# A capped mixture-of-experts stage: fp32 products replaced by high and low fp32r parts, with the rows stationary and a ring of 4 raw weights in place of 8

## The chip, the cores and the metric

The kernel runs on one core of one Trainium2 chip. The metric is the device time of one execution in microseconds (us); lower is better. The core has a matrix engine (TensorE, "PE" in the views, with its weight loads shown apart as "PEld"), three elementwise engines (VectorE "DVE", ScalarE "ACT", GpSimd "POOL") and a queue engine that only issues transfers ("SP", shown as "SPq"). Each engine works through its own list of instructions in order; semaphores make one wait for another.

## The reference

The program is a decoder of six blocks. The change touches one part of the third, the routed experts of `_moe_forward`. 2048 tokens pick 4 of 32 experts each, and an expert takes at most C = 80 rows (1.25 x 2048 / 32); what is over is dropped. What is computed for each expert is:

```python
D = 512
I = 256
E = 32
...
            Xp = x[slots_token].reshape(E, C, d)
            G = jnp.einsum('ecd,edi->eci', Xp, W_gate)
            U = jnp.einsum('ecd,edi->eci', Xp, W_up)
            Y = jnp.einsum('eci,eid->ecd', jax.nn.silu(G) * U, W_down)
```

## The kernel before

The decoder is a row of stages; each ends with a barrier of all engines. The stage here is `capped_experts` (names with the prefix `m_`). The stage ahead of it, `late_routing` (prefix `cd_`), finishes the routing, writes the picked rows to `packed` in DRAM, and runs a part of the shared expert. In its place in the program it also calls `load_first`, which issues the raw weights of the first R experts, so that they arrive during `late_routing`. The stage behind it, `combine` (prefix `cc_`), gathers the results.

In `capped_experts` an expert e passes through one slot on each engine:

- SP loads its 80 rows of x (160 KB, `packed` into `xe`, a piece of the tile `moe_base`), and its three weights, gate and up (128x1024 floats, 512 KB each) and down (512 KB), into a ring of R = 8 places; it stores the 80 result rows (160 KB, from `ye`, another piece of `moe_base`). A place of the ring is filled again when PE has finished the expert that used it (`pe_o`), line 2233.
- PE turns x with 4 transposes (L2292), multiplies in fp32 with the weights as the stationary operand: 8 products of 128x128 by 80 columns for gate, 8 for up (L2298), and then, for the expert before, 2 products of the stationary h (80 columns) by 512 columns of the down weight (L2307). Each fp32 product is two instructions in the trace.
- DVE copies the turned x out of the matrix engine's memory (PSUM) (L2271) and multiplies silu(gate) by up (L2279).
- ACT computes silu (L2257) and copies the result out (L2251).
- POOL does nothing in this stage.

The engines run one slot ahead or behind each other by the calls `following` and `preceding`; PE's slot is `turn_x(e+1)`, gate(e), up(e), `down(e-1)`.

A later stage, `routed_experts` (prefix `n_`, lines 2362 to 2600), is not changed. It works on tiles of 128 rows and already has the form that the change brings here: an fp32 operand is split into a high part (a copy into the type fp32r, "CAST") and a low part (operand minus high part, by `tensor_tensor` with `subtract`), and `split_product` (L77) makes three fp32r products of them: low by high (L81 or L82), high by low, high by high (L83). On DVE and POOL such a subtraction of weights reads two operands in SBUF, the on-chip memory; those of x and h read one in PSUM and one in SBUF. The rows of that stage are used below as a price list.

## Time and profile before

| what | value |
|---|---|
| median of three runs | 3454.94 us (3453.34 to 3456.48) |
| the profiled execution: its time, and its span in the trace | 3457.22 us, 3455.4 us |
| first row load of the changed stage issued | at 1513.14 us of the span |
| last result store issued, and its landing | 1703.0, about 1705 us |
| time from one expert to the next in its middle | 5.57 us |

All times inside the trace are counted from the start of the span; the run's time is 1.8 us longer than the span. PE's granted clock is given as a share of its full 2.4 GHz; it has two levels here, 0.50 (1.2 GHz) and 1.00. "DMA share" is the mean busy share of the core's 16 transfer engines, GB/s what they moved.

### The profile page before, as it was taken

The numbers are of one execution on the slowest core, as the hardware profiler recorded it, in microseconds if no ns is written. First come the engines' busy times: TensorE is split into PE (matmuls) and PEld (weight loads), VectorE is DVE, ScalarE is ACT, GpSimd is POOL, SyncE is SP. The second block draws the span as 40 slices with busy tenths as digits, with TensorE's granted clock in tenths as the row PEclk, the third lists the DMA queues.
The fourth block names the chain that finished last, engine by engine and source line by source line (L and its number), as shares of the span: only waits on it lengthen the run. The fifth ranks groups of instructions, "written<-read, shape, count | busy, mean of one in ns | idle before, by whom it ended". The sixth has DMA issues, their size and how long they took to land. (4 is left out here: it accounts for less than half of the span.)

```text
span 3455.4 us, 58053 instructions
## 1 busy us (share of the span) xinstructions
PE 3126.9 (90%) x20720; PEld 2609.3 (76%) x20720; DVE 2117.7 (61%) x3794; ACT 1291.1 (37%) x3291; POOL 1456.0 (42%) x1470
## 2 busy tenths in 40 slices
PE   7999999999969999799896999699999999869991
PEld 5887878878847777677674777488888888758881
DVE  5667566676636667521285777566666678645556
ACT  2343333333346666401212333244444444324430
POOL 4554443344422333310173222355555556444445
PEclk9999999999979999899997999799999999979996
DMA  4001016023410111249573112311101001156664
GB/s 171 18 13 57 0 36 233 0 78 109 151 33 26 45 33 62 93 154 342 164 166 107 40 43 58 126 32 35 35 11 49 11 24 45 43 200 223 224 222 158
DMA packets 137869, 317.13 MB, mean 92 GB/s; under 512 B 18425, under 2 KB 30457, under 8 KB 135538
## 3 DMA queue, kind: packets, MB, share of 16 engines
q1 hardware_dynamic: 120194, 274.61, 23.5%
q0 software_dynamic: 15360, 36.25, 4.0%
...
## 5 line engine op out<-in xcount | busy, mean ns | idle before, releaser
L398 POOL TENSOR_TENSOR a_sq<-a_tq,a_sinq 128x256 f32<-128x256 f32 x128 | 150.4, 1195 | 359.4 <-DVE a_tq L474 358.1
L398 POOL TENSOR_TENSOR a_sk<-a_tk,a_sink 128x256 f32<-128x256 f32 x128 | 123.9, 987 | 90.0 <-DVE a_tk L474 90.0
L364 ACT COPY a_probT<-bank 128x512 f32<-128x512 f32 x64 | 37.5, 586 | 329.0 <-PE bank L713 329.0
L411 POOL TENSOR_TENSOR e_sk<-e_tk 128x512 f32<-128x512 f32 x64 | 66.5, 1039 | 205.5 <-DVE e_tk L501 205.5
L353 ACT ACTIVATE e_prob<-bank,e_nb,e_rq 128x128 f32<-128x128 f32 x256 | 113.8, 455 | 86.6 <-DVE e_nb L575 86.6
L348 ACT ACTIVATE a_sm<-a_sm,a_nmax 128x128 f32<-128x128 f32 x256 | 99.9, 391 | 122.3 <-DVE a_nmax L570 122.3
L952 ACT ACTIVATE b_prob<-bank,b_nb 128x128 f32<-128x128 f32 x512 | 139.1, 386 | 13.6 <-DVE b_nb L1148 13.4
L1046 POOL TENSOR_TENSOR d_prob<-d_prob,d_nmax 128x1024 f32<-128x1024 f32 x32 | 63.9, 1998 | 181.5 <-DVE d_nmax L1143 181.5
L2478 POOL TENSOR_TENSOR n_wu_lo<-nw_wu,n_wu_hi 128x1408 fp32r<-128x1408 f32 x23 | 74.0, 3219 | 136.5 <-DVE n_wu_hi L2522 136.5
L496 DVE TENSOR_TENSOR a_kr<-a_kr,a_sk 128x512 f32<-128x512 f32 x64 | 66.5, 1039 | 89.0 <-POOL a_sk L398 89.0
L1145 DVE TENSOR_REDUCE b_nmax<-bank 128x8 f32<-128x1024 f32 x64 | 77.9, 1218 | 67.6 <-PE bank L1289 63.5
L81 PE MATMUL bank<-a_wq_hi,a_x_lo 128*128 128x512 f32 x256 | 107.4, 419 | 7.3 <-DVE a_wq_lo L214 7.2
L943 ACT COPY b_probT<-bank 128x512 f32<-128x512 f32 x128 | 78.3, 612 | 89.7 <-PE bank L1298 89.6
L81 PE MATMUL bank<-e_wo_hi,e_z_lo 128*128 128x512 f32 x256 | 107.4, 420 | 3.1 <-DVE e_z_lo L538 3.1
L81 PE MATMUL bank<-a_wo_hi,a_z_lo 128*128 128x512 f32 x256 | 106.1, 415 | 2.9 <-DVE a_z_lo L538 2.9
L386 POOL TENSOR_TENSOR a_x_lo<-a_xall,a_x_hi 128x512 fp32r<-128x512 f32 x64 | 89.8, 1403 | 41.4 <-ACT a_x_hi L320 41.4
L413 POOL TENSOR_TENSOR e_sq<-e_tq 128x512 f32<-128x512 f32 x64 | 66.6, 1040 | 96.4 <-DVE e_tq L505 96.4
L81 PE MATMUL bank<-a_wk_hi,a_x_lo 128*128 128x512 f32 x256 | 100.9, 394 | 6.7 <-DVE a_wk_lo L214 6.7
L364 ACT COPY e_probT<-bank 128x512 f32<-128x512 f32 x64 | 37.5, 586 | 180.0 <-PE bank L713 180.0
L572 DVE TENSOR_REDUCE e_nmax<-bank 128x4 f32<-128x512 f32 x64 | 44.2, 690 | 96.2 <-PE bank L697 96.2
L2483 POOL TENSOR_TENSOR n_wd_lo<-nw_wd,n_wd_hi 128x1024 fp32r<-128x1024 f32 (+1 forms) x46 | 85.4, 1876 | 39.5 <-ACT n_wd_hi L2451 39.5
L83 PE MATMUL bank<-e_wo_hi,e_z_hi 128*128 128x512 f32 x256 | 102.0, 399 | 0.0
...
## 6 DMA issues: line engine op xcount, KB each, us to landing
...
```

Of the source, the lines that this page charges most:

```text
L81: nc.tensor.matmul(ps, a_lo, b_hi, start=start, stop=False)
L83: return nc.tensor.matmul(ps, a_hi, b_hi, start=False, stop=stop)
L348: step = nc.scalar.activation(prob[:, j, :], sm[:, j, :], ACT.Exp, bias=nmax[:, j:j + 1], accum_out=rsum[:, j:j + 1])
L353: step = nc.scalar.activation(prob[:, j, :], pS[:, P * j:P * j + P], ACT.Exp, bias=nb[:, j:j + 1], scale=rq[:, par, j:j + 1], accum_out=rs ...
L364: nc.scalar.copy(probT[:], pP[:, :]).then_inc(act_pt, 1)
L386: sub = nc.gpsimd.tensor_tensor(x_lo[:, par].rearrange("p c t -> p (c t)"), xall[:, b, :], x_hi[:, par].rearrange("p c t -> p (c t)").bitc ...
L398: step = nc.gpsimd.tensor_tensor(o, i, s, ALU.mult)
L943: nc.scalar.copy(probT[:, s // 2 % 2, s % 2], pP[:, :]).then_inc(act_pt, 1)
L952: step = nc.scalar.activation(prob[:, p % 2, i], pS[:, i // H, P * (i % H):P * (i % H) + P], ACT.Exp, bias=nb[:, p % 2, i:i + 1], scale=SCALE)
L1145: nc.vector.tensor_reduce(nmax[:, p], scores, AX.X, ALU.max, negate=True).then_inc(v_nm, 1)
L2478: nc.gpsimd.tensor_tensor(lo["u"][:, w], raw["u"][:, w], hi["u"][:, w].bitcast(F32), ALU.subtract).then_inc(g_u, 1)
L2483: sub = nc.gpsimd.tensor_tensor(o, x, y.bitcast(F32), ALU.subtract)
```

## The change

- `CappedWeights` holds a ring of R = 4 places in place of 8. Gate and up stand side by side in one array (`in_c_wgu`), so that one transfer of 1 MB brings both (8 KB in a row for each partition, where it was twice 4 KB). `load_first` brings 4 experts.
- ACT copies both halves of the joined weight and the down weight into fp32r (three copies of 128x1024 for each expert), and also x, h and the results. DVE subtracts for the low parts of both halves, of x and of h. POOL subtracts for the low part of the down weight.
- PE holds the rows as the stationary operand (80 columns) and moves 512 columns of weight: `up` is 4 x 3 products, `down` 2 x 3. The result has rows on partitions, so h is turned by two transposes more (`turn_h`).
- The place of a weight in the ring is filled again once its low part is made (`v_up`, `g_down`), one slot earlier than PE's use of it.
- All slots are written out one by one (no loop on the chip). `gate` and `h` share one piece of `moe_base` (`spare`).

```diff
--- before.py
+++ after.py
@@ -2176,153 +2176,226 @@
 class CappedWeights:
 
 
-    NE, F, R = 32, 256, 8
+    NE, F, R = 32, 256, 4
 
     def __init__(self, st, w_dram):
         self.w_dram = w_dram
...
+        self.up = st.sbuf("up", [P, self.R, C, 2 * self.F])
+        self.down = st.sbuf("down", [P, self.R, self.F // P, D])
+        self.up_in = [st.sem(f"up_in{n}") for n in range(self.R)]
+        self.down_in = [st.sem(f"down_in{n}") for n in range(self.R)]
+
+    def load_up(self, sp, e):
+        n = e % self.R
+        sp.dma_start(self.up[:, n], self.w_dram["wgu"][e]).then_inc(self.up_in[n], 16)
+
+    def load_down(self, sp, e):
+        n = e % self.R
+        sp.dma_start(self.down[:, n], self.w_dram["wd"][e]).then_inc(self.down_in[n], 16)
 
     def load_first(self, sp):
...
+        for e in range(self.R):
+            self.load_up(sp, e)
+            self.load_down(sp, e)
+
+
+def capped_experts(nc, psum, ident, packed, result, zero, weights, xe, ye, spare):
 
     NE, CAP, F, R = weights.NE, 80, weights.F, weights.R
...
+    FC, HALF = F // P, C // 2
     with ExitStack() as ctx:
         st = Stage(nc, ctx, "m")
-        pX, pG, pU, pO = psum[0:2], psum[2:4], psum[4:6], psum[6:8]
...
+        pX, pU, pH, pO = psum[0:2], psum[2:4], psum[4:6], psum[6:8]
+        up_hi, up_lo = (st.sbuf(n, [P, 2, C, 2 * F], F32R) for n in ("up_hi", "up_lo"))
+        down_hi, down_lo = (st.sbuf(n, [P, 2, FC, D], F32R) for n in ("down_hi", "down_lo"))
+        x_hi, x_lo = (st.sbuf(n, [P, 2, C, CAP], F32R) for n in ("x_hi", "x_lo"))
+        gate = h = spare.rearrange("p (n f) -> p n f", n=2)
+        h_hi, h_lo = (st.sbuf(n, [P, FC, CAP], F32R) for n in ("h_hi", "h_lo"))
         x_in = [st.sem(f"x_in{n}") for n in range(R)]
         y_out = [st.sem(f"y_out{n}") for n in range(2)]
...
+        z_out, pe_x, pe_u, pe_h, pe_o = st.sems("z_out", "pe_x", "pe_u", "pe_h", "pe_o")
+        act_x, act_up, act_down, act_g, act_h, act_y = st.sems("act_x", "act_up", "act_down", "act_g", "act_h", "act_y")
+        v_x, v_up, v_h, v_hl, g_down = st.sems("v_x", "v_up", "v_h", "v_hl", "g_down")
         block = ctx.enter_context(nc.Block())
+
+        def part(half):
+            return slice(HALF * half, HALF * half + HALF)
 
         @block.sync
         def _(sp):
...
+            def load_x(e):
+                sp.dma_start(xe[:, e % R, :], packed[e]).then_inc(x_in[e % R], 16)
+
+            def store(e):
+                sp.wait_ge(act_y, done(e))
+                sp.dma_start(result[0:NE * CAP].rearrange("(e r) d -> e r d", r=CAP)[e], ye[:, e % 2, :]).then_inc(y_out[e % 2], 16)
+
+            def follow(e):
+                if e + R < NE:
+                    sp.wait_ge(pe_x, done(e))
+                    load_x(e + R)
+                    sp.wait_ge(v_up, done(2 * e + 1))
+                    weights.load_up(sp, e + R)
 
             for n in range(2):
                 sp.sem_inc(y_out[n], 16)
...
+            for e in range(R):
+                load_x(e)
             sp.dma_start(result[NE * CAP:NE * CAP + 1, :], zero[0:1, :]).then_inc(z_out, 16)
...
-                    sp.wait_ge(pe_o, done(R * i + n))
-                    load(i + 1, n)
...
+            follow(0)
+            for e in range(NE):
+                follow(e + 1)
+                if e + R < NE:
+                    sp.wait_ge(g_down, done(e))
+                    weights.load_down(sp, e + R)
+                if e:
+                    store(e - 1)
+            store(NE - 1)
             sp.wait_ge(z_out, 16)
             for n in range(2):
                 sp.wait_ge(y_out[n], landed(NE // 2))
 
         @block.scalar
         def _(act):
...
+            head_start(act, act_x, act_up, act_down, act_g, act_h, act_y)
+
+            def take_x(e):
+                act.wait_ge(pe_x, done(e))
+                if e >= 2:
+                    act.wait_ge(pe_u, done(2 * (e - 2) + 1))
+                nc.scalar.copy(x_hi[:, e % 2], pX[e % 2][:, 0:C * CAP].rearrange("p (c t) -> p c t", c=C)).then_inc(act_x, 1)
+
+            def split_up(e, half):
+                act.wait_ge(weights.up_in[e % R], landed(e // R))
+                if e >= 2:
+                    act.wait_ge(pe_u, done(2 * (e - 2) + half))
+                nc.scalar.copy(up_hi[:, e % 2, part(half)], weights.up[:, e % R, part(half)]).then_inc(act_up, 1)
+
+            def split_down(e):
+                act.wait_ge(weights.down_in[e % R], landed(e // R))
+                act.wait_ge(pe_o, done(e - 2))
+                nc.scalar.copy(down_hi[:, e % 2], weights.down[:, e % R]).then_inc(act_down, 1)
+
+            def take_h(e):
+                act.wait_ge(pe_h, done(e))
+                act.wait_ge(pe_o, done(e - 1))
+                nc.scalar.copy(h_hi[:], pH[e % 2][:, 0:FC * CAP].rearrange("p (c t) -> p c t", c=FC)).then_inc(act_h, 1)
+
+            def take_y(e):
                 act.wait_ge(pe_o, done(e))
...
+                act.wait_ge(y_out[e % 2], landed(e // 2))
+                nc.scalar.copy(ye[:, e % 2, :], pO[e % 2][0:CAP, :]).then_inc(act_y, 1)
+
+            for half in range(2):
+                split_up(0, half)
+            take_x(0)
+            for half in range(2):
+                split_up(1, half)
+            for e in range(NE):
+                if e + 1 < NE:
+                    take_x(e + 1)
+                split_down(e)
+                if e + 2 < NE:
+                    split_up(e + 2, 0)
+                act.wait_ge(pe_u, done(2 * e + 1))
+                act.wait_ge(pe_h, done(e - 2))
+                nc.scalar.activation(gate[:, e % 2], pU[e % 2][0:CAP, 0:F], ACT.Silu).then_inc(act_g, 1)
+                if e + 2 < NE:
+                    split_up(e + 2, 1)
+                take_h(e)
+                if e:
+                    take_y(e - 1)
+            take_y(NE - 1)
+
+        @block.gpsimd
+        def _(pool):
+            head_start(pool, g_down)
+            for e in range(NE):
+                pool.wait_ge(act_down, done(e))
+                nc.gpsimd.tensor_tensor(down_lo[:, e % 2], weights.down[:, e % R], down_hi[:, e % 2].bitcast(F32), ALU.subtract).then_inc(g_down, 1)
 
         @block.vector
         def _(dve):
...
-                nc.vector.tensor_copy(xT[:, n % 2], pX[n % 2][:, 0:C * CAP].rearrange("p (c t) -> p c t", c=C)).then_inc(v_x, 1)
...
+            head_start(dve, v_x, v_up, v_h, v_hl)
+
+            def take_x_lo(e):
+                dve.wait_ge(act_x, done(e))
+                nc.vector.tensor_tensor(x_lo[:, e % 2], pX[e % 2][:, 0:C * CAP].rearrange("p (c t) -> p c t", c=C),
+                                        x_hi[:, e % 2].bitcast(F32), ALU.subtract).then_inc(v_x, 1)
+
+            def split_up_lo(e, half):
+                dve.wait_ge(act_up, done(2 * e + half))
+                nc.vector.tensor_tensor(up_lo[:, e % 2, part(half)], weights.up[:, e % R, part(half)],
+                                        up_hi[:, e % 2, part(half)].bitcast(F32), ALU.subtract).then_inc(v_up, 1)
+
+            def take_h_lo(e):
+                dve.wait_ge(act_h, done(e))
+                nc.vector.tensor_tensor(h_lo[:], pH[e % 2][:, 0:FC * CAP].rearrange("p (c t) -> p c t", c=FC),
+                                        h_hi[:].bitcast(F32), ALU.subtract).then_inc(v_hl, 1)
+
+            split_up_lo(0, 0)
+            take_x_lo(0)
+            split_up_lo(0, 1)
+            split_up_lo(1, 0)
+            for e in range(NE):
+                if e:
+                    take_h_lo(e - 1)
+                if e + 1 < NE:
+                    take_x_lo(e + 1)
+                    split_up_lo(e + 1, 1)
                 dve.wait_ge(act_g, done(e))
...
+                nc.vector.tensor_tensor(h[:, e % 2], gate[:, e % 2], pU[e % 2][0:CAP, F:2 * F], ALU.mult).then_inc(v_h, 1)
+                if e + 2 < NE:
+                    split_up_lo(e + 2, 0)
+            take_h_lo(NE - 1)
 
         @block.tensor
         def _(pe):
...
+            head_start(pe, pe_x, pe_u, pe_h, pe_o)
+
+            def turn_x(e):
+                pe.wait_ge(x_in[e % R], landed(e // R))
+                pe.wait_ge(v_x, done(e - 2))
                 for c in range(C):
...
+                    last = nc.tensor.transpose(pX[e % 2][:, CAP * c:CAP * c + CAP], xe[:, e % R, P * c:P * c + P], ident[0:CAP, 0:CAP])
                 last.then_inc(pe_x, 1)
 
-            def up(ps, w, n, sem):
+            def up(e):
+                pe.wait_ge(v_x, done(e))
+                pe.wait_ge(v_h, done(e - 2))
+                for c in range(C):
+                    if c % HALF == 0:
+                        pe.wait_ge(v_up, done(2 * e + c // HALF))
+                    last = split_product(nc, pU[e % 2][0:CAP, :], x_hi[:, e % 2, c, :], x_lo[:, e % 2, c, :],
+                                         up_hi[:, e % 2, c, :], up_lo[:, e % 2, c, :], start=c == 0, stop=c == C - 1)
+                    if c % HALF == HALF - 1:
+                        last.then_inc(pe_u, 1)
+
+            def turn_h(e):
+                pe.wait_ge(v_h, done(e))
+                pe.wait_ge(v_hl, done(e - 2))
                 for f in range(FC):
-                    for c in range(C):
-                        last = nc.tensor.matmul(ps[n % 2][:, CAP * f:CAP * f + CAP], w[:, n, c, P * f:P * f + P],
-                                                xT[:, n % 2, c, :], start=c == 0, stop=c == C - 1)
...
+                    last = nc.tensor.transpose(pH[e % 2][:, CAP * f:CAP * f + CAP], h[:, e % 2, P * f:P * f + P], ident[0:CAP, 0:CAP])
+                last.then_inc(pe_h, 1)
+
+            def down(e):
+                pe.wait_ge(v_hl, done(e))
+                pe.wait_ge(g_down, done(e))
                 pe.wait_ge(act_y, done(e - 2))
                 for f in range(FC):
...
+                    last = split_product(nc, pO[e % 2][0:CAP, :], h_hi[:, f, :], h_lo[:, f, :],
+                                         down_hi[:, e % 2, f, :], down_lo[:, e % 2, f, :], start=f == 0, stop=f == FC - 1)
                 last.then_inc(pe_o, 1)
 
...
-                pe.wait_ge(w_in[n], 48 * (i + 1))
...
+            turn_x(0)
+            for e in range(NE):
+                if e + 1 < NE:
+                    turn_x(e + 1)
+                up(e)
+                if e:
+                    down(e - 1)
+                turn_h(e)
+            down(NE - 1)
 
 
 class RoutedWeights:
@@ -2874,7 +2947,7 @@
                 weights = CappedWeights(Stage(nc, routed, "cw"), w)
                 late_routing(nc, "cd", psum, router, weight, early, weights.load_first)
                 capped_experts(nc, psum, ident, packed1.rearrange("(e r) d -> e r d", r=80), result1, zero, weights,
-                               base[0:80, B - weights.R:B], base[0:80, EARLY:EARLY + 2])
+                               base[0:80, B - weights.R:B], base[0:80, EARLY:EARLY + 2], base[0:80, EARLY + 2])
             combine(nc, "cc", base, result1, router.rows, weight, x2, 4, rest, staged_d.fetch)
         narrow_attention(nc, "d", banks, ident, lambda b: steps[0][b], lambda b: steps[1][b], of("d_"), 16, PLAN_4, staged_d, head_d, causal=True, ahead=fetch_e)
         with ExitStack() as moe:
@@ -2983,7 +3056,7 @@
     return {
         "c_rw": by_chunk(i["L0_ffn_router_w"].T), "c_sg": by_chunk(i["L0_ffn_shared_gate"].T),
         "c_su": by_chunk(i["L0_ffn_shared_up"].T), "c_sd": by_chunk(i["L0_ffn_shared_down"].T),
...
+        "c_bias": i["L0_ffn_e_bias"], "c_iota": iota, "c_wgu": by_expert(np.concatenate([i["L0_ffn_W_gate"], i["L0_ffn_W_up"]], axis=2)),
         "c_wd": by_expert(i["L0_ffn_W_down"]),
         "f_rw": by_chunk(i["L1_ffn_gate_w"].T), "f_iota": iota, "f_wg": by_expert(i["L1_ffn_gate_proj"].transpose(0, 2, 1)),
         "f_wu": by_expert(i["L1_ffn_up_proj"].transpose(0, 2, 1)), "f_wd01": by_expert(down[:, :2 * P]),
```

The order of the instructions shows three places. First DVE, from the start of the stage on; before, it has two short instructions for each expert (`m_xT` the turned x, `m_h` the product with silu).

```order
-L2271 COPY m_xT<-bank 128x320 x2
-L2279 TENSOR_TENSOR m_h<-m_gate,bank 128x160
...
-L2271 COPY m_xT<-bank 128x320
-L2277 REGISTER_ALU
-L2279 TENSOR_TENSOR m_h<-m_gate,bank 128x160
```

In the changed kernel it has five (`m_up_lo` is a half of the low part of gate and up, `m_x_lo` and `m_h_lo` those of x and h, `moe_base<-moe_base,bank` the product with silu).

```order
1006 L2347 TENSOR_TENSOR moe_base<-moe_base,bank 80x256
1007 L2328 TENSOR_TENSOR m_up_lo<-cw_up,m_up_hi 128x1024
1008 L2333 TENSOR_TENSOR m_h_lo<-bank,m_h_hi 128x160
1009 L2323 TENSOR_TENSOR m_x_lo<-bank,m_x_hi 128x320
1010 L2328 TENSOR_TENSOR m_up_lo<-cw_up,m_up_hi 128x1024
1011 L2347 TENSOR_TENSOR moe_base<-moe_base,bank 80x256
```

So the second half of the low part of expert e+1 stands ahead of the product of expert e. Next ACT, in one slot in the middle of the changed stage (before it has the silu and the copy of the result alone).

```order
597 L2266 CAST m_x_hi<-bank 128x320
598 L2277 CAST m_down_hi<-cw_down 128x1024
599 L2272 CAST m_up_hi<-cw_up 128x1024
600 L2302 ACTIVATE moe_base<-bank 80x256
601 L2272 CAST m_up_hi<-cw_up 128x1024
602 L2282 CAST m_h_hi<-bank 128x160
603 L2287 COPY moe_base<-bank 80x512
```

Three large copies came in, two of them ahead of the silu and one behind it. Last SP, where the first weights are loaded and the stage begins; first before (the loads of the eight experts, of which the last stands here), then of the change.

```order
-L2190 DMA cw_wg<-in_c_wg 128x1024
-L2190 DMA cw_wu<-in_c_wu 128x1024
-L2190 DMA cw_wd<-in_c_wd 128x1024
...
 L1912 UNCONDITIONAL_BRANCH
-L2214 UNCONDITIONAL_BRANCH
-L2217 DMA moe_base<-packed 80x512 x8
-L2230 DMA result<-all_zero 1x512
```

```order
142 L2224 UNCONDITIONAL_BRANCH
143 L2227 DMA moe_base<-packed 80x512 x4
144 L2244 DMA result<-all_zero 1x512
145 L2227 DMA moe_base<-packed 80x512
146 L2190 DMA cw_up<-in_c_wgu 128x2048
147 L2227 DMA moe_base<-packed 80x512
148 L2190 DMA cw_up<-in_c_wgu 128x2048
149 L2194 DMA cw_down<-in_c_wd 128x1024
150 L2227 DMA moe_base<-packed 80x512
```

The weights of experts 4 and on are now issued from the first slot on, where before expert 8 waited for the end of expert 0.

## Rows read from the trace of the kernel before

**Rows 1.** The page: span, and busy time of each engine.

```profile
span 3455.4 us, 58053 instructions
PE 3126.9 (90%) x20720; PEld 2609.3 (76%) x20720; DVE 2117.7 (61%) x3794; ACT 1291.1 (37%) x3291; POOL 1456.0 (42%) x1470
```

**Rows 2.** Busy time by stretch: the loads ahead, then the stage in four parts.

```profile
core 0: us, PE busy (x) PEld busy (x) DVE busy (x) ACT busy (x) POOL busy (x), PEclk, DMA share, GB/s
1455.00:1480.00 25.00, 22.93 (x144) 20.61 (x144) 9.14 (x42) 3.44 (x6) 11.67 (x12) 0.81 1.03 396
1513.00:1533.00 20.00, 17.34 (x79) 15.89 (x80) 2.12 (x5) 0.61 (x2) 0.00 (x0) 0.57 0.25 67
1535.00:1560.00 25.00, 25.00 (x186) 20.46 (x185) 3.25 (x8) 3.84 (x9) 0.00 (x0) 1.00 0.98 321
1560.00:1670.00 110.00, 110.00 (x789) 87.53 (x788) 16.26 (x40) 17.69 (x40) 0.00 (x0) 1.00 1.00 341
1670.00:1702.00 32.00, 32.00 (x217) 24.24 (x216) 3.89 (x10) 5.00 (x11) 0.00 (x0) 1.00 0.11 35
```

**Rows 3.** Timeline of PE over one expert: start, duration, instruction.

```profile
1561.53 0.44 PE L2292 MATMUL bank<-all_ident,moe_base 80*128 80x80 f32 x4
1561.81 1.95 PE L2298 MATMUL bank<-m_xT,cw_wg 128*128 128x80 f32 x16
1563.59 1.95 PE L2298 MATMUL bank<-m_xT,cw_wu 128*128 128x80 f32 x16
1565.38 1.88 PE L2307 MATMUL bank<-cw_wd,m_h 128*80 128x512 f32 x4
1567.10 0.30 PE L2292 MATMUL bank<-all_ident,moe_base 80*128 80x80 f32 x2
```

**Rows 4.** Issues of the stage's small transfers, KB each, median us to landing.

```profile
moe_base<-packed SPq DMA_DIRECT2D x32, 160.0 KB, 5.7
result<-moe_base SPq DMA_DIRECT2D x32, 160.0 KB, 8.4
```

**Rows 5.** Timeline of PE in the stage with prefix n_: split products.

```profile
3161.89 0.39 PE L82 MATMUL bank<-n_wd_lo,n_h_hi 128*128 128x512 f32 x1
3162.12 0.40 PE L83 MATMUL bank<-n_wd_hi,n_h_hi 128*128 128x512 f32 x1
3162.35 0.39 PE L81 MATMUL bank<-n_wd_hi,n_h_lo 128*128 128x512 f32 x1
```

**Rows 6.** Groups by shape: busy us, mean ns; idle before and releaser.

```profile
L2450 ACT CAST n_wd_hi<-nw_wd 128x1024 fp32r<-128x1024 f32 x23 | 24.4, 1062 | 0.0
L2433 ACT CAST n_x_hi<-bank 128x512 fp32r<-128x512 f32 x46 | 27.0, 586 | 152.9 <-PE bank L2555 152.9
L2438 ACT CAST n_h_hi<-bank 128x256 fp32r<-128x256 f32 x46 | 16.9, 368 | 3.8 <-PE bank L2562 3.8
L2459 ACT ACTIVATE n_gate<-bank 128x352 f32<-128x352 f32 x46 | 21.4, 464 | 65.0 <-PE bank L83 65.0
L2251 ACT COPY moe_base<-bank 80x512 f32<-80x512 f32 x32 | 18.6, 581 | 105.8 <-PE bank L2307 80.9 <-DMA result<-moe_base 24.8
L2500 DVE TENSOR_TENSOR n_x_lo<-bank,n_x_hi 128x512 fp32r<-128x512 f32 x46 | 31.8, 691 | 33.5 <-ACT n_x_hi L2433 33.4
L2505 DVE TENSOR_TENSOR n_h_lo<-bank,n_h_hi 128x256 fp32r<-128x256 f32 x46 | 19.2, 418 | 35.3 <-ACT n_h_hi L2439 35.3
L2483 POOL TENSOR_TENSOR n_wd_lo<-nw_wd,n_wd_hi 128x1024 fp32r<-128x1024 f32 x23 | 56.7, 2464 | 39.5 <-ACT n_wd_hi L2451 39.5
```

**Rows 7.** Timelines of POOL and DVE, n_ stage: two pairs that overlap.

```profile
3107.06 3.24 POOL L2478 TENSOR_TENSOR n_wu_lo<-nw_wu,n_wu_hi 128x1408 fp32r<-128x1408 f32 x1 [5.56 <-DVE n_wu_hi L2522]
3108.66 3.12 DVE L2517 TENSOR_TENSOR n_wg_lo<-nw_wg,n_wg_hi 128x1408 fp32r<-128x1408 f32 x1
3292.15 3.22 POOL L2478 TENSOR_TENSOR n_wu_lo<-nw_wu,n_wu_hi 128x1408 fp32r<-128x1408 f32 x1 [5.55 <-DVE n_wu_hi L2522]
3294.50 2.35 DVE L2517 TENSOR_TENSOR n_wg_lo<-nw_wg,n_wg_hi 128x1408 fp32r<-128x1408 f32 x1
```

**Rows 8.** Timeline of ACT, n_ stage: instructions back to back.

```profile
3152.77 0.37 ACT L2438 CAST n_h_hi<-bank 128x256 fp32r<-128x256 f32 x1
3153.02 0.28 ACT L2439 CAST n_h_hi<-bank 96x128 fp32r<-96x128 f32 x1
3153.18 1.06 ACT L2450 CAST n_wd_hi<-nw_wd 128x1024 fp32r<-128x1024 f32 x1
```

82 lines of the change are left out of this document (removed).

## The prediction

> **What bounds the kernel now.** I read the page first [rows 1]: PE is busy for 90% of the span, which says only that a change of PE's work can count. Then the busy time by stretch over the changed stage [rows 2]. The reader is to see that from 1535 to 1702 us PE is busy in every microsecond at the full clock, while DVE and ACT have 16 and 18 us of work in 110. The first 20 us are different: the clock stands at 0.57 of full on the mean, that is mostly at 1.2 GHz, behind the idle time at the barrier. The timeline of one expert [rows 3] shows PE with no gap: transposes 0.28 us, gate 1.78, up 1.79, down 1.72, and the next expert starts 5.57 us after this one. So the stage is bound by PE.
>
> The same rows show a second thing that is nearly full. From 1560 to 1670 us the DMA share is 1.00 at 341 GB/s. An expert moves 3 x 0.524 MB of weights and 2 x 0.164 MB of rows, 1.90 MB, and 1.90 / 5.57 us is 341 GB/s. The issues [rows 4] show that a row load of 160 KB lands after 5.7 us and a store after 8.4: they stand behind weights. PE never waits for a weight only because a ring of 8 lies in between. The transfers can do more where they carry weights alone (396 GB/s at share 1.03, 1455 to 1480 us) and did less at 321 [rows 2].
>
> **What PE's work costs after.** Six fp32 groups go; 12 + 6 products of 512 columns come. Such a product in the n_ stage starts 0.23 us after the one before it [rows 5]; 18 of them are 4.14 us. The x transposes stay at 0.28, the two of h are half of that, 0.14. With some 0.2 for restarts after a change of type (an estimate: the nearest row is none, so 0 to 0.4), PE needs 4.75 us for an expert, 0.82 less than 5.57. If nothing else bound, 32 x 0.82 = 26 us would go. That is the upper end of what can be gained.
>
> **What ACT does after** [rows 6]. Three copies of 128x1024 at 1.06 are 3.19. For x (320 columns) and h (160) I go along the line through 586 ns at 512 and 368 ns at 256 (0.85 ns a column): 0.42 and 0.29. Silu of 256 columns, between 464 ns at 352 and less: 0.38. The copy of the result 0.58. Together 4.86; but an instruction with nothing to wait for starts some 0.11 before the end of the one ahead (3153.18 + 1.06 against the next at 3154.13; [rows 8] show 3153.02 under 3152.77 + 0.37), so 7 of them hold the engine for about 4.1. ACT fits under 4.75.
>
> **What DVE and POOL do after, and each to the other.** The low parts of x and h have an operand in PSUM: 0.49 and 0.32 by the line through 691 and 418 ns; the product 0.42. The low parts of weights have both in SBUF. [Rows 7] show the same 128x1408 subtraction with 3.12 and with 2.35 us. The first runs beside POOL's for 3107.06 + 3.24 - 3108.66 = 1.64 us, the second for 3292.15 + 3.22 - 3294.50 = 0.87; 3.12 - 1.64 and 2.35 - 0.87 are both 1.48. So DVE gets nothing done there while POOL's subtraction runs, and then needs 1.48. For 1024 columns that is 1.08, with the start-up of 0.15 that the 691 ns for 512 columns leave at the same rate 1.23. POOL's own instruction takes 2.46 on the mean, 2.38 undisturbed. The Trainium skill says the same under "SBUF — State Buffer", section "SBUF: two separate sides": the pair of ports that both use is an exclusive lock for a whole instruction, taken by a DVE instruction with two SBUF inputs too; by that rule a DVE sum without the lock would be too small, and the trace agrees.
>
> DVE alone needs 2 x 1.23 + 0.49 + 0.32 + 0.42 = 3.7. If POOL's 2.38 falls wholly on it, 6.1; if it starts just when DVE turns to x and h (0.8 of cover), 5.3. What is queued behind it decides: the second half of the next expert's low part stands ahead of this expert's product with silu, for that product PE's `turn_h` waits, and for PE everything. In a slot of 4.75 there is room: after silu(e) DVE has the product, half one, h and x, half two, 3.7 in all, and POOL's subtraction can only start after ACT's copy of the down weight, about 3.2 us behind the silu (1.06 + 0.29 + 0.58 + 0.42 + 1.06 less the overlaps). Walking two slots with these numbers: in the first POOL finds DVE on half two, starts at 3.8 and ends at 6.2, so the next slot's half one starts about 1 us late, h and x follow, and there POOL comes first: half two starts after it, some 2.4 late, and that slot grows by 1 to 1.5 us. Then it begins again. Slots of 4.75 and of 5.8 to 6.0 in turn: 5.3 on the mean. I take 5.3; the bounds are 4.75 (POOL always in a gap) and 5.75 (it falls into the chain each time).
>
> **The transfers after.** The bytes of an expert are the same, in rows of 8 KB for two thirds of the weights. 28 experts' weights instead of 24 now move inside the stage: 28 x 1.573 + 32 x 0.328 = 54.5 MB, 160 us at 341 GB/s. They start 4 us into the stage, not 21, and a stage of 32 x 5.3 = 170 us holds them; they bind first at 54.5 / 170 = 320 GB/s, which the row 1535 to 1560 just reaches (321). I cost them at nothing in the sum and keep 300 to 396 GB/s as the bounds. The stores lie behind more waiting bytes than before, and ACT must have them landed two experts later (10.6 us against 8.4 measured): narrow, but enough. The lighter `load_first` takes 6.3 MB out of the stretch 1455 to 1480, where PE works on the shared expert; I find no wait there that I can price and take 0, at most 2 us gained. The loop written out costs nothing by itself: other stages of this program are written out too.
>
> **The sum.** Before, the stage runs from 1513.1 (first row load) to 1705 (last store landed), 191.9 us. After:
> - rows land at about 1515.5; transposes at the low clock, x_hi 0.42, x_lo 0.49 and the way between them: first product at 1517.5;
> - to about 1533 PE has the low clock, as now. 15.5 us at 2 x 4.56 an expert is 1.7 experts;
> - 30.3 experts at 5.3: 160.6 us, to 1693.6;
> - the last expert's h parts (0.29 + 0.32 and the ways), down 1.38, copy 0.58, store and landing 2.3: 5.7 us, to 1699.3.
>
> That is 5.7 us before 1705. The profiled execution took 3457.2 and would take 3451.5; it lies 2.3 above the median of the runs, so the median comes to 3454.9 - 5.7 = 3449.2. I say 3449. A measurement of this kernel tells 0.2%, 6.9 us, from no change: the likeliest time lies just inside that.
>
> **The rivals.**
> - POOL's subtraction mostly finds a gap (half two is ready early, and the ways between engines may shift the phase). Then PE's 4.75 holds: 30.3 x 0.55 = 16.7 less, 22 us gained in all; but 54.5 MB at 341 from 1517 on end at 1677, and the last expert needs two slots and the end, some 14 us more: 1691, 14 us gained. 3441, down to 3433 if transfers run near 396. For it: DVE has 3.7 of 4.75. Chance 0.25.
> - It finds the chain each time: 5.75 an expert, 30.3 x 0.45 = 13.6 more than the sum, 8 us slower than before, 3463. That is the case on the other side; it decides when the mean slot passes 5.5. Chance 0.15.
> - The transfers fall to 300 GB/s, because row stores and loads mix with more queued weights: 182 us from 1517 is 1699, and about 9 for the last expert: 1708, 3 us slower; at 290, 9 slower. 3458 to 3464. Against it: 341 over 110 us, and larger rows. Chance 0.10.
> - The sum's own case, 5.15 to 5.5 an expert: 4 us more to 6 us less than said, 3444 to 3455. Chance 0.50.
>
> **How the numbers follow.** Within 0.2% are 3448.0 to 3461.9. Of the sum's case 0.20 lies below that, 0.30 inside; of the first rival 0.23 below, 0.02 inside; of the second 0.05 inside, 0.10 above; of the third 0.05 and 0.05. Faster 0.43, same 0.42, slower 0.15; I move 0.04 from same to slower for what the written-out code and the shared port may do beyond these cases: 0.43, 0.38, 0.19. The range goes from 3434 (most of the first rival) to 3464 (the upper ends of the other two).
>
> **What would show it.** Right: PE busy near 90% of the stage, split products 0.23 apart, the halves of the low part at 1.23 alone and up to 3.5 us beside POOL, in turns; PE's idle time in front of `turn_h`, released by the product on DVE; first result slots at the low clock as before. Wrong: PE waiting for `up_lo` behind a late weight (the transfers bind), ACT waiting long for a landed store, POOL's instruction far from 2.4, the clock falling to 1.2 GHz in the middle because of PE's waits (then 9 us an expert, and all of this is void), or slots of one length, 4.75 or 5.75.

## The result, and the profile after

| what | before | after |
|---|---|---|
| median (lowest to highest) of 6 runs each | 3454.88 us (3452.93 to 3458.06) | 3439.23 us (3435.96 to 3442.04) |
| ratio, 95% interval | | 0.9958 (0.9946 to 0.997) |
| profiled execution, its span | 3457.22, 3455.4 us | 3438.98, 3436.8 us |

The changed kernel is faster by 15.7 us in the medians, 10 to 19 us by the interval: twice to three times the 5.7 us forecast, inside the range, below the likeliest case's own 3444 to 3455. Of the runs told of below, one of the six of e11_change_again took 4008 us at a granted clock of 0.73; such an execution is left out of every median and ratio here. The two profiled executions are 18.6 us of span apart. Put down by stretch, with the issues of SP as marks (the first weight load, the first row load, the last result store, the load of `d_wo` in the stage behind `combine`):

| stretch | before | after | difference |
|---|---|---|---|
| start to the first weight load | 1448.9 | 1447.1 | -1.8 |
| to the first row load (`late_routing`) | 64.2 | 61.2 | -3.0 |
| to the last result store (`capped_experts`) | 189.9 | 173.7 | -16.2 |
| to the load of `d_wo` in the next stage | 145.7 | 146.2 | +0.5 |
| the rest | 1606.7 | 1608.5 | +1.8 |

Below, "the stage" is the third row, and "a slot" is the time from one expert's silu on ACT to the next one's, read from the timeline of ACT. The page after, against [rows 1]:

```profile
span 3436.8 us, 57141 instructions
PE 3093.7 (90%) x20208; PEld 2559.9 (74%) x20208; DVE 2239.6 (65%) x3890; ACT 1400.5 (41%) x3451; POOL 1550.9 (45%) x1502
```

It says little: PE has 33 us less to do, the other three have 95 to 122 us more, nearly all of it beside PE. The busy time by stretch says more (columns as in [rows 2]):

```profile
1510.00:1515.00 5.00, 3.48 (x13) 2.39 (x14) 3.55 (x4) 3.70 (x6) 0.00 (x0) 0.59 0.48 139
1515.00:1520.00 5.00, 4.08 (x17) 2.34 (x16) 3.13 (x5) 3.43 (x6) 3.31 (x1) 0.72 1.00 347
1520.00:1525.00 5.00, 5.00 (x27) 3.37 (x26) 4.00 (x6) 4.46 (x8) 2.98 (x1) 1.00 0.96 357
1560.00:1650.00 90.00, 80.34 (x415) 52.64 (x414) 83.75 (x88) 74.72 (x122) 49.60 (x18) 1.00 1.01 367
```

Two things are to be seen. In the middle of the stage PE is no longer the full engine: it is busy for 80.3 of 90 us, DVE for 83.8. And the clock is full from about 1517.8 on (the 0.72 of the second row is 0.50 up to there and 1.00 behind it), some 9 us after the first row load; before, it was full at 1532.9, 20 us after ([rows 2] show 0.57 from 1513 to 1533). The waits between 1505 and 1700 us name who waits for whom (engine and line, what it waited for: us in total, times, longest):

```profile
POOL m_down_lo L2315 <- ACT m_down_hi L2277: 104.7, 32, 34.1
PE bank L2378 <- DVE moe_base L2347: 17.0, 11, 1.6
DVE moe_base L2347 <- ACT moe_base L2302: 13.5, 21, 2.5
PE bank L2360 <- DMA moe_base<-packed: 4.4, 1, 4.4
```

PE waits 11 times in the 31 slots, up to 1.6 us, at `turn_h` (L2378) for DVE's product with silu (L2347). No row has PE or ACT waiting for a weight or a store. The slots are 4.57, 4.57 and 6.39 us, again and again: 5.18 on the mean (5.14 in the table of the runs, which takes in the first and last slots). One long slot in the timeline of DVE:

```profile
1600.61 0.42 DVE L2347 TENSOR_TENSOR moe_base<-moe_base,bank 80x256 f32<-80x256 f32 x1 [0.70 <-ACT moe_base L2302]
1600.95 2.31 DVE L2328 TENSOR_TENSOR m_up_lo<-cw_up,m_up_hi 128x1024 fp32r<-128x1024 f32 x1
1603.81 1.21 DVE L2328 TENSOR_TENSOR m_up_lo<-cw_up,m_up_hi 128x1024 fp32r<-128x1024 f32 x1
1605.19 0.42 DVE L2347 TENSOR_TENSOR moe_base<-moe_base,bank 80x256 f32<-80x256 f32 x1 [0.17 <-ACT moe_base L2302]
1605.52 2.84 DVE L2328 TENSOR_TENSOR m_up_lo<-cw_up,m_up_hi 128x1024 fp32r<-128x1024 f32 x1
...
1608.92 3.00 DVE L2328 TENSOR_TENSOR m_up_lo<-cw_up,m_up_hi 128x1024 fp32r<-128x1024 f32 x1
1611.84 0.41 DVE L2347 TENSOR_TENSOR moe_base<-moe_base,bank 80x256 f32<-80x256 f32 x1
```

And of POOL, over the same time:

```profile
1599.28 2.89 POOL L2315 TENSOR_TENSOR m_down_lo<-cw_down,m_down_hi 128x1024 fp32r<-128x1024 f32 x1 [3.98 <-ACT m_down_hi L2277]
1603.86 3.42 POOL L2315 TENSOR_TENSOR m_down_lo<-cw_down,m_down_hi 128x1024 fp32r<-128x1024 f32 x1 [1.68 <-ACT m_down_hi L2277]
1608.43 2.41 POOL L2315 TENSOR_TENSOR m_down_lo<-cw_down,m_down_hi 128x1024 fp32r<-128x1024 f32 x1 [1.15 <-ACT m_down_hi L2277]
```

POOL's instruction ends at 1602.17, 1607.28 and 1610.84; DVE's halves beside it end at 1603.26, 1608.36 and 1611.92, each 1.08 to 1.09 us later. Where DVE was first (1603.81 against 1603.86), DVE takes 1.21 and POOL 3.42, that is 2.4 and the 1.0 that it stood. In the first slot half two just slips in ahead of POOL. In the second everything is shifted by what POOL took from half one, POOL comes first, half two ends at 1611.92, and the product behind it starts 2.1 us after silu has ended (silu from 1609.34 for 0.38, in the timeline of ACT). That is the long slot. After it POOL's work falls where DVE has time, and the cycle begins again. The groups of these instructions (busy us, mean ns | idle time ahead of them, releaser):

```profile
L2328 DVE TENSOR_TENSOR m_up_lo<-cw_up,m_up_hi 128x1024 fp32r<-128x1024 f32 x64 | 122.3, 1912 | 2.3 <-ACT m_up_hi L2272 2.3
L2315 POOL TENSOR_TENSOR m_down_lo<-cw_down,m_down_hi 128x1024 fp32r<-128x1024 f32 x32 | 92.7, 2897 | 104.7 <-ACT m_down_hi L2277 104.7
L2272 ACT CAST m_up_hi<-cw_up 128x1024 fp32r<-128x1024 f32 x64 | 66.9, 1049 | 10.5 <-PEq L50 10.0 <-PE bank L83 0.4
L2347 DVE TENSOR_TENSOR moe_base<-moe_base,bank 80x256 f32<-80x256 f32 x32 | 13.2, 413 | 13.6 <-ACT moe_base L2302 13.5
```

### The profile page after: what moved, and what is told of

Same layout as the page of the kernel before. It is cut to its first block and busy times, and to the rows that moved or that the text cites. A ratio compares the mean times of both kernels' runs of the same rounds, so it can differ in the third digit from the quotient of the medians.

```text
span 3436.8 us, 57141 instructions
## 1 busy us (share of the span) xinstructions
PE 3093.7 (90%) x20208; PEld 2559.9 (74%) x20208; DVE 2239.6 (65%) x3890; ACT 1400.5 (41%) x3451; POOL 1550.9 (45%) x1502
## 5 line engine op out<-in xcount | busy, mean ns | idle before, releaser
L2315 POOL TENSOR_TENSOR m_down_lo<-cw_down,m_down_hi 128x1024 fp32r<-128x1024 f32 x32 | 92.7, 2897 | 104.7 <-ACT m_down_hi L2277 104.7
L2328 DVE TENSOR_TENSOR m_up_lo<-cw_up,m_up_hi 128x1024 fp32r<-128x1024 f32 x64 | 122.3, 1912 | 2.3 <-ACT m_up_hi L2272 2.3
```

What stands on the lines that cost most here:

```text
L2315: nc.gpsimd.tensor_tensor(down_lo[:, e % 2], weights.down[:, e % R], down_hi[:, e % 2].bitcast(F32), ALU.subtract).then_inc(g_down, 1)
L2328: nc.vector.tensor_tensor(up_lo[:, e % 2, part(half)], weights.up[:, e % R, part(half)], up_hi[:, e % 2, part(half)].bitcast(F32), ALU.sub ...
```

## The experiments

All with their profiles; each ratio is to the kernel before on the same chip, with its 95% interval. "Rows" is the stretch from the first weight load to the first row load.

| run | median us | ratio (interval) | rows | stage | mean slot |
|---|---|---|---|---|---|
| the change | 3439.23 | 0.9958 (0.9946 to 0.997) | 61.2 | 173.7 | 5.14 |
| e1_no_down_lo | 3429.97 | 0.9947 (0.993 to 0.9964) | 61.2 | 168.3 | 4.97 |
| e2_halves_together | 3427.74 | 0.9948 (0.9931 to 0.9964) | 61.3 | 168.0 | 4.94 |
| e3_down_on_dve | 3429.82 | 0.9945 (0.9926 to 0.9964) | 61.1 | 171.8 | 5.09 |
| e4_before_ring4 | 3452.46 | 1.0011 (1.0 to 1.0022) | 61.0 | 191.5 | 5.74 |
| e5_fp32_rows | 3445.22 | 0.9983 (0.9974 to 0.9993) | 61.1 | 186.8 | 5.54 |
| e6_rows_4k | 3435.63 | 0.9956 (0.9939 to 0.9973) | 61.1 | 173.7 | 5.14 |
| e7_quarter_loads | 3414.10 | 0.9899 (0.988 to 0.9918) | 61.1 | 155.3 | 4.55 |
| e8_quarter_change | 3432.42 | 0.9948 (0.9929 to 0.9967) | 61.4 | 173.7 | 5.14 |
| e9_four_results | 3428.76 | 0.9918 (0.9905 to 0.9931) | 63.9 | 162.9 | 4.79 |
| e10_halves_again | 3436.73 | 0.9937 (0.9921 to 0.9953) | 63.7 | 169.0 | 4.97 |
| e11_change_again | 3439.72 | 0.9955 (0.9942 to 0.9968) | 63.6 | 173.0 | 5.13 |
| e12_before_again | one run, 3455.0 | | 63.8 | 190.3 | 5.71 |

The kernel before had a median of 3447.0, 3449.7 and 3456.7 us in the three groups e1 to e4, e5 to e8 and e9 to e11, so medians of different groups don't compare; the stage does, since it repeats to about 1 us (173.7 and 173.0, 168.0 and 169.0, 189.9 and 190.3). Three of the runs leave out a part of the work (e1, e7 and e8; each says which) and show only where time goes.

The slots themselves tell more than their mean. From the timelines of ACT:

```
the change            4.32 4.58 4.56 6.41 4.56 4.57 6.39 4.57 4.57 6.39 ...
e1_no_down_lo         4.31 4.57 4.57 4.56 4.57 4.57 4.56 4.57 5.08 5.13 5.24 5.33 ... 6.48 ...
e2_halves_together    4.33 4.57 4.57 4.57 4.56 4.57 4.57 5.37 5.17 5.12 4.95 5.00 ...
e3_down_on_dve        4.31 4.57 4.56 4.57 4.57 5.07 5.39 5.29 5.35 5.29 5.24 5.27 ...
e5_fp32_rows          4.99 5.57 5.57 5.57 5.57 5.57 5.57 ...
e7_quarter_loads      4.32 4.57 4.56 4.57 4.56 4.57 ... (to the end)
e8_quarter_change     4.32 4.57 4.56 6.41 4.56 4.57 6.41 4.56 4.57 6.39 ...
e9_four_results       4.34 4.57 4.56 (12 more like these) 5.00 5.01 4.99 4.88 ... 5.45 5.29
```

### Is it the shared port?

The first theory was the prediction's own: POOL's subtraction takes time from DVE, and what stands behind half two on DVE is late. e1_no_down_lo leaves POOL's subtraction out: the low part of the down weight isn't made, and the product that used it takes the high part once more. Where PE and SP waited for the low part (`g_down`) they now wait for ACT's copy (`act_down`), so the down weight's place in the ring is also free earlier.

```diff
-                nc.gpsimd.tensor_tensor(down_lo[:, e % 2], weights.down[:, e % R], down_hi[:, e % 2].bitcast(F32), ALU.subtract).then_inc(g_down, 1)
...
-                                         down_hi[:, e % 2, f, :], down_lo[:, e % 2, f, :], start=f == 0, stop=f == FC - 1)
+                                         down_hi[:, e % 2, f, :], down_hi[:, e % 2, f, :], start=f == 0, stop=f == FC - 1)
```

> The changed kernel without POOL's subtraction: the low part of the down weight is left out and its product is made with the high part again, so TensorE has the same work and POOL has none. Theory: slots of 6.39 us come from POOL holding the port against DVE. Then every slot is 4.57 us, the halves of the low part all take 1.21 us, and 31 x (5.14 - 4.57) = 17.7 us go: 3421 to 3426, against 3439 of the changed kernel. Rival, transfers bind: 54.5 MB at the 370 GB/s of the changed kernel are 147 us, and the stage's 173.7 us shrink by 10 to 13 only, with waits of ACT for weights: 3427 to 3430. Rival, the long slot has another cause (ACT's order): no change, 3439.

Every half took 1.21 to 1.23 us, and the pattern with a long third slot is gone; but after eight slots of 4.57 or under they went up to mostly 4.9 to 5.5, one to 6.48, in which ACT waited 2.23 us for a landed store. The stage fell by 5.4 us, not by the 17.7 of the theory nor the 10 to 13 of its first rival, and ACT now waited 19.3 us for landed stores.

e2_halves_together keeps all the work and moves DVE's: product, both halves of expert e+2, then the low parts of h and x. So nothing that PE needs soon stands right behind a half.

```diff
+            split_up_lo(1, 1)
+            take_x_lo(1)
             for e in range(NE):
-                if e:
-                    take_h_lo(e - 1)
-                if e + 1 < NE:
-                    take_x_lo(e + 1)
-                    split_up_lo(e + 1, 1)
...
                     split_up_lo(e + 2, 0)
+                    split_up_lo(e + 2, 1)
+                take_h_lo(e)
+                if e + 2 < NE:
+                    take_x_lo(e + 2)
```

> The changed kernel with DVE's order in a slot changed: product with silu, half one and half two of the low part of the expert two ahead, then the low parts of h and x. Theory: POOL's subtraction (2.4 us) and the two halves (2.4 us) share one port; side by side the halves leave POOL the time of h, x and the product, nothing behind a half is urgent, and the slots become even at 4.57 to 4.8: 8 to 17 us less than the changed kernel, 3422 to 3431. Rival, the sum of all port time is what counts (4.8 of 5.14 us): 3434 to 3439. Rival, the low part of h now comes too late for the down products: slower than 3439.

The long slots went here too: seven slots at 4.57 or under, then 4.95 to 5.4, and the stage fell by 5.7 us. Its waits show the same new one; e10_halves_again repeated it (stage 169.0):

```profile
ACT moe_base L2287 <- DMA result<-moe_base: 18.6, 22, 1.1
PE bank L2378 <- DVE moe_base L2344: 6.6, 20, 0.9
```

e3_down_on_dve gives the down weight's subtraction to DVE, behind the others, so POOL is idle in the stage.

```diff
...
+                dve.wait_ge(act_down, done(e))
+                nc.vector.tensor_tensor(down_lo[:, e % 2], weights.down[:, e % R], down_hi[:, e % 2].bitcast(F32), ALU.subtract).then_inc(g_down, 1)
```

> The changed kernel with the subtraction for the down weight moved from POOL to DVE, last in each slot. DVE then has 3 x 1.21 + 0.47 + 0.31 + 0.42 = 4.83 us of work and no port to share; less the overlap at each start about 4.5. Theory (port lock): slots of 4.57 to 4.8 us, 3421 to 3432, all of them even. Rival (DVE's total counts, waits for silu and h add to it): 5.1 to 5.5 us a slot, 3438 to 3450.

DVE has 3 x 1.21 + 0.49 + 0.31 + 0.42 = 4.85 us an expert, less some 0.1 by which each of the six overlaps the next: the first five slots of 4.57 show that this fits. Then they went to 5.3, the rival's size, but e1 with less for DVE to do went there too, and ACT waited 23.7 us for landed stores here. The stage is 1.9 us shorter than the change's: POOL's help, 2.4 us of work that stops DVE for nearly as long, is worth nothing in this order.

### Or late bytes?

In all three, what came next looked like the transfers. e8_quarter_change is the change itself with the loads of experts 4 to 31 cut to a quarter (three quarters of each weight are then an earlier expert's); e7_quarter_loads does the same to e2_halves_together.

```diff
-        sp.dma_start(self.up[:, n], self.w_dram["wgu"][e]).then_inc(self.up_in[n], 16)
+        part = slice(0, C if e < self.R else 1)
+        sp.dma_start(self.up[:, n, part], self.w_dram["wgu"][e][:, part]).then_inc(self.up_in[n], 16)
...
```

> The changed kernel's own order with the same quarter loads (three quarters of the weights of experts 4 to 31 are those of an earlier expert). Theory: its slots of 4.57, 4.57 and 6.39 us in turn come from POOL's subtraction against DVE's alone: the pattern and the mean of 5.1 to 5.2 stay, and with them a stage of 170 to 174 us. Rival: the long slots are late weights, or the wait for them: then they shrink with the bytes, mean below 4.8 and a stage below 162.

> The order with both halves of DVE's low part behind the product (the run e2_halves_together), and the loads of experts 4 to 31 cut to a quarter of their bytes, so that three quarters of each of their weights are those of an earlier expert. Theory: the 5.1 us slots in the second part of e2_halves_together are those of the transfers alone. Then all slots are 4.5 to 4.6 us and the stage takes 152 to 156 us, some 13 us less than there. Rival: DVE and POOL still collide in this order: slots of 4.57 and longer ones in turn, mean above 4.8, stage above 160.

Both theories held. The change with a quarter of the bytes has the same stage to 0.1 us and the same slots, so in the change the transfers cost nothing. In the other order all slots are 4.57: PE busy in every microsecond. First the busy time of e8_quarter_change, then of e7_quarter_loads, over the same stretch:

```profile
1560.00:1640.00 80.00, 71.96 (x371) 46.90 (x369) 74.66 (x79) 67.07 (x109) 45.86 (x16) 1.00 0.46 142
```

```profile
1560.00:1640.00 80.00, 80.00 (x420) 53.77 (x419) 69.03 (x89) 75.61 (x124) 42.09 (x18) 1.00 0.51 158
```

The two kernels differ in the order of DVE's list alone, and their stages are 173.7 and 155.3 us. So DVE and POOL together have room for 4.57 us; the order, not the sum of the work, made the long slots. And from 4.57 to the 5.1 of e2_halves_together it is the bytes, or the places of the ring or of the results that wait for them. e9_four_results asks which: four places for result rows (the smaller ring of x leaves them free) in e2_halves_together.

```diff
-        y_out = [st.sem(f"y_out{n}") for n in range(2)]
+        y_out = [st.sem(f"y_out{n}") for n in range(4)]
...
-            act.wait_ge(y_out[e % 2], landed(e // 2))
+            act.wait_ge(y_out[e % 4], landed(e // 4))
...
-                               base[0:80, B - weights.R:B], base[0:80, EARLY:EARLY + 2], base[0:80, EARLY + 2])
+                               base[0:80, B - weights.R:B], base[0:80, 8:12], base[0:80, EARLY + 2])
```

> The order of e2_halves_together with four places for result rows in place of two, so that ACT's copy waits for the store of four experts ago. Theory: in e2_halves_together the second part is bound by the rate of the transfers, 1.90 MB an expert at about 370 GB/s, 5.1 us. Then ACT's wait for a landed store goes (18.6 us there), but PE or ACT waits for late weights instead, and slots stay at 5.0 to 5.2, stage 166 to 169 us, time within 2 us of e10. Rival: it was the latency of two result places (a landing of 9.5 us against two slots of 4.57), and the transfers have room left: slots near 4.6 to 4.8, stage 155 to 162, 6 us or more under e10.

> The kernel of e2_halves_together once more, on the chip of the next run and of e9. Expected: stage 166 to 170 us as before, 5 to 6 us under e11 in the stage; in the whole time 3 to 8 us under it, ratio to before 0.992 to 0.996.

> The changed kernel once more, as the measure for the two ahead of it. Expected: stage 173.7 us and slots of 4.57, 4.57, 6.39 as before, ratio to before 0.9946 to 0.997.

The two repeats came out 4.0 us apart in the stage (169.0 and 173.0), not 5 to 6; e11 has one slot of 6.00 right behind its first and then the cycle of 4.57, 4.57 and 6.40. For e9 neither theory was right by itself. The stage came to 162.9, 6.1 below e10: fifteen slots stayed at 4.57 or under where e10 had eight, and ACT waits for no store any more. So that part was the two result places. Then weights were late, as the waits of e9_four_results show:

```profile
ACT m_up_hi L2272 <- DMA cw_up<-in_c_wgu: 11.5, 14, 1.4
PE bank L2378 <- DVE moe_base L2344: 5.4, 11, 0.9
```

Its busy time by stretch has the transfers as full as in any run of this stage:

```profile
1560.00:1640.00 80.00, 78.01 (x404) 50.75 (x403) 61.46 (x84) 70.90 (x118) 39.69 (x18) 1.00 1.02 376
1640.00:1665.00 25.00, 22.42 (x115) 13.95 (x114) 15.64 (x23) 20.72 (x35) 11.11 (x5) 1.00 1.02 377
```

1.90 MB at 376 GB/s are 5.06 us, and from the sixteenth on its slots are mostly 4.8 to 5.5. The small transfers of e9 landed later than the change's (row loads 11.3 us after issue against 7.0, stores 11.6 against 6.9, medians), so more was queued. That speaks for the rate of the transfers as what binds there; a longer ring of weights beside it was not tried, so it is not shown. This kernel leaves nothing out and beats both the change and e10: 0.9918 against the change's 0.9955 on the same chip, 11 us in the medians, 10.1 in the stage.

e6_rows_4k asks whether the 8 KB rows made the transfers faster than the 341 GB/s of before: each load of gate and up as two transfers with 4 KB rows.

```diff
-        sp.dma_start(self.up[:, n], self.w_dram["wgu"][e]).then_inc(self.up_in[n], 16)
+        for c in (0, 2):
+            sp.dma_start(self.up[:, n, c:c + 2], self.w_dram["wgu"][e][:, c:c + 2]).then_inc(self.up_in[n], 16)
```

> The changed kernel with each 1 MB load of gate and up as two transfers of 512 KB, 4 KB in a row instead of 8. If the longer rows let the transfers run at 367 GB/s where they ran at 341 before, this one falls towards 341: an expert's 1.90 MB then needs 5.57 us, slots of 5.4 to 5.6, a stage of 178 to 182 us, about 6 us slower than the changed kernel. Rival: 341 was only what the slots of 5.57 us asked for, the transfers reach 365 with rows of either length: slots of 5.1 to 5.2, stage 173 to 175, the time within 2 us of the changed kernel's.

The rival held: the stage is the same to 0.1 us, and the busy time by stretch has

```profile
1560.00:1640.00 80.00, 70.33 (x366) 45.95 (x365) 74.68 (x78) 65.27 (x106) 44.28 (x16) 1.00 1.03 364
```

364 GB/s with 4 KB rows. The 341 of [rows 2] was what slots of 5.57 us asked for (1.90 / 5.57), and a DMA share of 1.00 beside it didn't mean a limit.

### What the orientation did, and the clock

e5_fp32_rows has the change's shape (rows stationary, gate and up side by side, ring of 4) with fp32 products and no high and low parts.

```diff
-                    last = split_product(nc, pU[e % 2][0:CAP, :], x_hi[:, e % 2, c, :], x_lo[:, e % 2, c, :],
-                                         up_hi[:, e % 2, c, :], up_lo[:, e % 2, c, :], start=c == 0, stop=c == C - 1)
+                    last = nc.tensor.matmul(pU[e % 2][0:CAP, :], xT[:, e % 2, c, :], weights.up[:, e % R, c, :], start=c == 0, stop=c == C - 1)
```

> The change's orientation (rows stationary, gate and up side by side, ring of 4) but with fp32 products as before: no high and low parts, no subtraction on DVE or POOL. Two fp32 down products of 512 columns took 1.72 us before [rows 3], so six take 5.16; with transposes of 0.28 and 0.14 and the way through silu a slot of 5.6 to 5.7 us is expected, and a stage of 184 to 190 us: the orientation alone gives nothing against 5.57, and the whole gain is that of fp32r. Rival: the orientation itself gives part of it, slots under 5.4. On the first stretch: if the clock rises late because of small fp32 products (as before, low until 1532), six wide fp32 products should bring it to full by about 1520, as the change does; if it is the type fp32r that counts, it stays low until about 1530.

The slot is 5.57, exactly that of before, so the orientation gives nothing in the steady part. But the stage is 3.0 to 3.4 us shorter (against the two profiles of the kernel before), 2.0 to 2.4 of it up to the third silu and 1.0 at its end. PE in e5_fp32_rows:

```profile
1508.68 1.37 PE L2288 MATMUL bank<-all_ident,moe_base 80*128 80x80 f32 x8 [4.09 <-DMA moe_base<-packed]
1510.06 6.34 PE L2296 MATMUL bank<-cw_up,m_xT 128*80 128x512 f32 x8
1517.79 3.60 PE L2296 MATMUL bank<-cw_up,m_xT 128*80 128x512 f32 x8
```

And in e12_before_again:

```profile
1512.20 3.62 PE L2298 MATMUL bank<-m_xT,cw_wg 128*128 128x80 f32 x16
1515.62 3.62 PE L2298 MATMUL bank<-m_xT,cw_wu 128*128 128x80 f32 x16
...
1522.98 3.62 PE L2298 MATMUL bank<-m_xT,cw_wu 128*128 128x80 f32 x16
1526.39 3.01 PE L2307 MATMUL bank<-cw_wd,m_h 128*80 128x512 f32 x4
```

The granted clock is the column behind POOL's; first e5, then e12_before_again:

```profile
1510.00:1515.00 5.00, 4.99 (x7) 1.63 (x7) 0.50 (x2) 0.00 (x0) 0.00 (x0) 0.50 0.01 2
1515.00:1520.00 5.00, 4.08 (x15) 1.55 (x14) 0.91 (x2) 0.67 (x2) 0.00 (x0) 0.95 0.49 162
```

```profile
1526.00:1528.00 2.00, 2.00 (x5) 0.91 (x5) 0.32 (x1) 0.00 (x0) 0.00 (x0) 0.50 0.00 0
1528.00:1530.00 2.00, 2.00 (x12) 1.16 (x10) 0.28 (x1) 0.47 (x1) 0.00 (x0) 0.84 0.00 0
```

With products of 80 columns PE worked without a pause from 1512 to 1526 at 1.2 GHz (16 of them from 1512.20 to 1515.62, 3.42 us, where [rows 3] have 1.79 at the full clock), and the group of the first wide products, from 1526.39 on, is the one in which the clock rose: it took 2.85 to the next instruction, where [rows 3] have 1.72. With wide products from the start (e5) the granted clock was 0.50 from 1510 to 1515 and 0.95 from 1515 to 1520. In the change, with fp32r products of 512 columns, it is much the same: they stood 0.43 apart from 1513.5, and 0.23 behind 1517.8.

```profile
1516.94 0.63 PE L81 MATMUL bank<-m_up_hi,m_x_lo 128*80 128x512 f32 x1
1517.37 0.58 PE L82 MATMUL bank<-m_up_lo,m_x_hi 128*80 128x512 f32 x1
1517.79 0.39 PE L83 MATMUL bank<-m_up_hi,m_x_hi 128*80 128x512 f32 x1
...
1520.28 0.39 PE L81 MATMUL bank<-m_up_hi,m_x_lo 128*80 128x512 f32 x1
1520.51 0.39 PE L82 MATMUL bank<-m_up_lo,m_x_hi 128*80 128x512 f32 x1
```

The type isn't what counts here, and the change of orientation is. (e5 changes the order of PE's work with the shape, so it is not shown that the width alone does it.)

### The ring of 4, and the stretch ahead

e4_before_ring4 is the kernel before with `R = 4`.

```diff
-    NE, F, R = 32, 256, 8
+    NE, F, R = 32, 256, 4
```

> The kernel before with its ring of 8 weights cut to 4 and nothing else. Theory for the 3.0 us that the stage ahead of the experts got shorter: 6.3 MB fewer loads beside it. Then that stretch shrinks by 3 us here too. In the expert stage a load of 1.57 MB has 4 slots, 22 us, against some 9 to land: slots stay 5.57 us, and the whole is 3452 (3450 to 3455). Rival: loads of experts 4 to 7 come late, TensorE waits: 3460 and more. Rival: the 3 us are chance, 3455.

In the stage the smaller ring costs before's order 1.2 to 1.6 us: some slots of 5.7 to 6.2, with PE's weight load waiting for late rows of x (17.8 us in total). No engine waits in it for an expert's weights to land. The stretch ahead took 61.0 us against 64.2 and seemed to show that lighter first loads are worth 3 us. Then e9, e10 and e11, with rings of 4 too, had 63.6 to 63.9. So the kernel before was profiled once more.

> The kernel of before, unchanged, for a second profile. The stretch from the first weight load to the first row load took 64.2 us in its first profile, 61.0 to 61.4 in eight profiles of kernels with a ring of 4 and 63.6 to 63.9 in three others. Theory: it has two lengths, whatever the kernel, and the ring of 8 adds at most 0.5 us: this profile shows about 61.5 or about 64. Rival: the heavier first loads stretch it by 3 us beyond that: 64.2 again if the short form, about 66.5 if the long one. The stage itself is expected at 189.9 us and the first result slots at 7.4 and 8.0, as before.

It took 63.8. That alone would suit both theories, but the timeline of PE tells the forms apart. In e12_before_again there are pauses with no releaser inside rows of small products:

```profile
1466.49 0.27 PE L1536 MATMUL bank<-all_ident,moe_xall 128*128 128x128 f32 x1 [0.29 <-issue]
1467.20 0.54 PE L1536 MATMUL bank<-all_ident,moe_xall 128*128 128x128 f32 x3 [0.44 <-issue]
1481.56 1.40 PE L1543 MATMUL bank<-cd_sxT,all_staged 128*128 128x128 f32 x11 [0.45 <-issue]
```

and in e10_halves_again, with a ring of 4, at the same places:

```profile
1469.51 0.27 PE L1536 MATMUL bank<-all_ident,moe_xall 128*128 128x128 f32 x1 [0.67 <-issue]
1483.85 1.16 PE L1543 MATMUL bank<-cd_sxT,all_staged 128*128 128x128 f32 x8 [0.38 <-issue]
```

The change's first profile has none. The pauses come to 1.0 to 1.9 us in the long profiles (0.2 to 0.9 each), so they are a part of the 2.4 to 3.0 us, not all of it. So the stretch has two lengths, 61.0 to 61.4 (nine profiles, where the expectation says eight) and 63.6 to 64.2 (five), in executions of the very same kernel (61.2 and 63.6 for the change), and within the long one the ring of 8 adds at most 0.6 us. Two profiles of two with a ring of 8 were long and three of twelve with a ring of 4; whether the lighter loads make the long form rarer stays open, and so does what causes it.

## Why the prediction was right and where it was off

- **PE bounds the kernel now: right.** Six wide fp32 products give a slot of 5.57 as well (e5), and with less for PE to do the same bytes went through in 5.18.
- **PE needs 4.75: it was 4.57.** All 18 products stood 0.23 apart as [rows 5] said; the 0.2 for restarts was 0.04 (one gap of 0.27 after the transposes). This term had an open end down to 0, and 0.18 of it wasn't there.
- **ACT fits: right.** 74.72 us in 90 are 4.3 for each 5.18, and e7 ran at 4.57 with it.
- **The shared port: right in mechanism, a little large.** DVE's half ended 1.08 us after POOL's instruction, as [rows 7] gave. The walk said 4.75 and 5.8 to 6.0 in turn, 5.3 on the mean; it was two of 4.57 and one of 6.39, 5.18. That the means are so near is in part luck: the long slot grew by 1.8 us, not 1 to 1.5, but came every third time, not every second; 4.57 and 6.39 in turn would be 5.48. The Trainium skill ("SBUF — State Buffer", section "SBUF: two separate sides") has the port pair as an exclusive lock for a whole instruction; the trace agrees from the other side too, POOL's 3.42 us with DVE ahead of it.
- **The transfers cost nothing: right** (e8). But the first rival's bound from them was taken at 341 GB/s, "54.5 MB at 341 from 1517 on end at 1677". 341 was a demand, not a limit; e9 ran at 376. And "PE never waits for a weight only because a ring of 8 lies in between" does not hold: e4, with a ring of 4, has no such wait either.
- **Lighter `load_first`, 0 to 2 us gained: 0 was about right.** The 3.0 us between the two profiles can't be put down to the change: its own two profiles have 61.2 and 63.6.
- **The step that failed: "to about 1533 PE has the low clock, as now."** The sum cost it as 15.5 us for 1.7 experts, 6.5 us more than at 5.3 each. The clock was full by 1517.8, 4.8 us after the first product instead of 15.5 (e5: 5.4 us after it). I took the stretch over unchanged from before, though the change alters just what PE does in it.

The stage can be put down by these. From the first row load to the first silu it took 2.5 us more than before (7.32 and 9.83; before, that silu needed only the gate's half). The first two slots took 8.90 instead of 15.48, the other 29 took 150.5 instead of 161.2, the end 1.3 less: -16.2. The forecast had 29 x (5.56 - 5.3), 7.5, for the steady part and lost 1.8 elsewhere. So 3.3 of the 10.5 us that were missing are the slot's size, and some 7 the start, of which the clock is about 4.3 (6.5 forecast; measured, eleven products at 0.43 instead of 0.23, 2.2); of the other 2.9, 1.7 is that the first two slots were both short (8.90 us, where two of 5.3 are 10.6), and the rest I can't put down.

The measured time is the one given for the first rival, 3441, but not by its mechanism: POOL did not find a gap, PE waited for DVE in every third slot. The sum's case held, with a mean slot of 5.18 in its 5.15 to 5.5, and its time was too high by the start.
